# A stacked fp16 null-value product and a three-pass fp16 decay product in a two-layer gated cross-attention kernel

## What is computed

```
# block 1: attention over 256 context rows and one null row
nk = jnp.broadcast_to(null_kv[0], (b, HEADS, 1, DH))
nv = jnp.broadcast_to(null_kv[1], (b, HEADS, 1, DH))
k = jnp.concatenate((nk, k), axis=-2)
v = jnp.concatenate((nv, v), axis=-2)
attn = jax.nn.softmax(jnp.einsum('bhid,bhjd->bhij', q * scale, k), axis=-1)
out = jnp.einsum('bhij,bhjd->bhid', attn, v)
out = jnp.einsum('bnf,fd->bnd', out.transpose(0, 2, 1, 3).reshape(b, -1, INNER), Wout)
...
# block 3: a first-order recurrence over the context rows, then a pick by the token's boundary count
a = jnp.exp(dt[:, :, None] * A[None, None, :])
u = (dt * bcoef)[:, :, None, None] * x4
_, s = jax.lax.associative_scan(comb, (a_b, u), axis=1)
depool_out = depool[jnp.arange(bsz)[:, None], plug]
h = jnp.einsum('bld,ed->ble', rmsnorm(embeds, g_res), W_in) + b_in
return depool_out + h
```

## Time and profile before

| | |
|---|---|
| median of three runs | 1682.9 us (1676.08 to 1683.25) |
| the profiled execution | 1678.45 us, span of the core 1676.7 us |
| TensorE (PE) busy | 1493.0 us, 89% |
| VectorE (DVE) busy | 1195.3 us, 71% |
| ScalarE (ACT) busy | 922.1 us, 55% |
| GpSimd (POOL) busy | 589.2 us, 35% |
| mean granted TensorE clock | 0.964 of full |
| one full step | 74.4 us (ScalarE's copy of p0T at 510.76, 585.17, 659.53 us) |

### The profile page before, as it was taken

The page is one execution under the profiler, slowest core; times in us unless marked ns, Lnnn a source line. Parts: engine busy times, 40 slices in busy tenths (PEclk is TensorE's granted clock), DMA queues, the critical chain, the costliest instruction groups (busy, mean ns, idle before and its releaser), DMA issues.

```text
span 1676.7 us, 35791 instructions
## 1 busy us (share of the span) xinstructions
PE 1493.0 (89%) x12510; PEld 1085.1 (65%) x12510; DVE 1195.3 (71%) x3240; ACT 922.1 (55%) x2526; POOL 589.2 (35%) x775
## 2 busy tenths in 40 slices
PE   3799999999999999999999999999765499999994
PEld 2567676767767676767767676776553266666662
DVE  5478788888878888887978888887763344445442
ACT  4276666767666676767666676766641133333331
POOL 3011333242323333232333324232333356555552
PEclk9899999999999999999999999999877699999997
DMA  7201021020202012020201102010400363333334
GB/s 249 70 1 64 14 64 58 20 77 2 77 8 71 26 52 71 7 76 1 77 14 64 65 14 77 2 58 8 164 32 0 105 173 61 60 59 58 58 61 123
DMA packets 77836, 98.12 MB, mean 59 GB/s; under 512 B 20400, under 2 KB 61376, under 8 KB 77600
## 3 DMA queue, kind: packets, MB, share of 16 engines
q1 hardware_dynamic: 51152, 77.01, 14.1%
q0 software_dynamic: 15680, 18.69, 6.8%
q10 hardware_dynamic: 10832, 0.13, 0.3%
HBM read 64.89 MB, written 35.10 MB: 60 GB/s over the span
## 4 chain that ended last, share of the span: by engine, by line
PE 62%; DVE 18%; ACT 7%; POOL 5%; issue 3%; SPq 2%; DMA 2%; ACTq 0%; POOLq 0%; DVEq 0%
PE S L1282 11%; PE W L949 9%; PE W L951 9%; PE W L950 9%; PE T L954 7%; PE O L1302 6%; PE O L1053 4%; POOL routing_table L693 4%; PE S L1027 3%; DVE mx L1462 3%; ACT prob L785 2%; DVE pTl L1474 2%; PE W L954 2%; PE W L1158 2%; PE W L1138 2%
## 5 line engine op out<-in xcount | busy, mean ns | idle before, releaser
L785 ACT ACTIVATE prob<-S,nm 128x256 f32<-128x256 f32 x512 | 235.5, 474 | 80.8 <-DVE nm L1465 54.1
L778 ACT ACTIVATE pTh<-T 128x512 f16<-128x512 f32 x256 | 139.3, 597 | 137.1 <-PE T L954 136.9
L634 POOL TENSOR_SCALAR ve_ln<-mv_ln 128x2 f32<-128x2 f32 x64 | 14.6, 229 | 472.8 <-DVE mv_ln L1436 471.9
L1462 DVE TENSOR_REDUCE mx<-S 128x2 f32<-128x512 f32 x256 | 163.3, 679 | 21.2 <-PE S L1027 20.7
L1282 PE MATMUL S<-GL,xgh 128*128 x568 | 169.8, 381 | 2.7 <-DVE xgl L1756 2.7
L1474 DVE SCALAR_TENSOR_TENSOR pTl<-T,pTh 128x512 f16<-128x512 f32 x256 | 164.1, 682 | 6.4 <-ACT pTh L778 6.4
L716 POOL DMA_INDIRECT acc_rows<-ysb,tab x71 | 112.3, 1582 | 134.2 <-DMA acc_rows<-ysb,tab 90.3
L794 ACT ACTIVATE prob<-prob,rden 128x256 f32<-128x256 f32 x256 | 116.5, 504 | 56.4 <-DVE p0n L1483 55.7
L954 PE MATMUL T<-ident,prob 128*128 128x128 f32 x1024 | 141.5, 282 | 1.8 <-DVE prob L1487 1.7
L949 PE MATMUL W<-cTh,Wkh 128*128 128x256 f16 x512 | 140.6, 275 | 0.0
L950 PE MATMUL W<-cTl,Wkh 128*128 128x256 f16 x512 | 140.5, 274 | 0.0
(11 more groups left out here) (293 smaller groups left out, 4325.1 us busy)
## 6 DMA issues: line engine op xcount, KB each, us to landing
cx<-in_ctx_dram SPq DMA_DIRECT2D x16, 512.0 KB
gst<-in_L_ffn_gating_w_dram SPq DMA_DIRECT2D x16, 512.0 KB
gating_split<-gsp SPq DMA_DIRECT2D x16, 512.0 KB
GL<-gating_split SPq DMA_DIRECT2D x8, 1024.0 KB
stg<-in_L_xattn_Wkv_dram SPq DMA_DIRECT2D x8, 512.0 KB, 13.5
xl<-in_x_dram SPq DMA_DIRECT2D x16, 256.0 KB
lst<-in_L_ffn_linear_w_dram SPq DMA_DIRECT2D x16, 256.0 KB
xres<-in_x_dram SPq DMA_DIRECT2D x16, 256.0 KB
```

Of the source, the lines that this page charges most:

```text
L778: A(flat(pTh[:, h, :, :]), T[h][:, :], ACT.Copy).then_inc(s_pTh[h], 1)
L785: ins = A(prob[:, h, t, :], S[h][:, t * NTOK:(t + 1) * NTOK], ACT.Exp, bias=nm[:, h, t:t + 1], scale=SM, accum_out=rs[:, h, t:t + 1])
L1462: ins = V.tensor_reduce(mx[:, h, :], S[h][:, :].rearrange("p (t k) -> p t k", t=TT), AX.X, ALU.max)
```

## The change

It does five things.

1. **Null product.** `Wnv` and `p0T` become fp16 with 96 rows: in rows 0, 32 and 64 start the high, low and high probabilities, against the high, high and low of Wnv. One fp16 matmul does what the fp32 product did. `p0n` has its 16 columns three times (96 wide, zeros between), the transposes give 96 rows, ScalarE copies all 96 rounded to fp16, and VectorE then overwrites rows 32 to 47 with the remainder. The bank is now freed by VectorE.
2. **Decay product.** `dec` and `u` are split into fp16 high and low by GpSimd (two instructions each, per batch), and the fp32 products become `mm3`. win_unit waits for the splits.
3. `u` is one buffer; its split goes into two pairs of buffers. VectorE waits for the former split before it writes `u`.
4. `x4` shares the buffer of `xh`, `x4T` that of `xn`. VectorE's wait for the former x4 rows' DMA moves from j = 7 to j = 2.
5. In setup: larger zero fills on GpSimd, four more small VectorE copies, and `Wnv` made by two VectorE instructions in place of one.

```
-         ("p0T", False, POST)
+         ("p0T", True, POST)
...
+                    wait_apart(pool, s_gt, post.n + 1)
+                    link(pool.tensor_copy(dech[:, :, :], dec[:, :, :]))
+                    pool.tensor_tensor(decl[:, :, :], dec[:, :, :], dech[:, :, :], ALU.subtract).then_inc(s_gts, 1)
                     rstd_of("ln4", post, 1e-5).then_inc(s_rstd["ln4"], 1)
                     wait_apart(pool, s_rstd["ln4"], post.n + 1)
                     rms_of_normed("ln4", 1e-6).then_inc(s_rms, 1)
+                if PRE in parts:
+                    wait_apart(pool, s_u, nxt.n + 1)
+                    link(pool.tensor_copy(uh[nxt.par][:, :, :], u[:, :, :]))
+                    pool.tensor_tensor(ul[nxt.par][:, :, :], u[:, :, :], uh[nxt.par][:, :, :], ALU.subtract)\
+                        .then_inc(s_us, 1)
...
                     if j == 0 and post_:
-                        whole("p0T", p0T[:, :])
+                        one_of("p0T", p0T[:, :])
...
-                        ins = tr(o[0:HEADS, t * P:(t + 1) * P], p0n[post.par][:, t, :])
+                        ins = tr(o[0:NULL_ROWS, t * P:(t + 1) * P], p0n[post.par][:, t, :])
...
-                    pe.wait_ge(s_gt, post.n + 1)
-                    pe.wait_ge(s_u, post.n + 1)
+                    pe.wait_ge(s_gts, post.n + 1)
+                    pe.wait_ge(s_us, post.n + 1)
...
-                            ins = M(o[:, c], dec[:, k, tok], u[post.par][:, k, :], start=False, stop=(k == 1))
+                            ins = mm3(o[:, c], dech[:, k, tok], decl[:, k, tok], uh[post.par][:, k, :],
+                                      ul[post.par][:, k, :], False, k == 1)
...
-            V.tensor_scalar(Wnv[:, :], banks_of[12][0:HEADS, 0:D], WS, None, ALU.mult).then_inc(s_init, 1)
+            link(V.tensor_scalar(Wnv[:, :], banks_of[12][0:NULL_ROWS, 0:D], WS, None, ALU.mult))
+            V.scalar_tensor_tensor(Wnv[64:64 + HEADS, :], banks_of[12][64:64 + HEADS, 0:D], WS, Wnv[64:64 + HEADS, :],
+                                   ALU.mult, ALU.subtract).then_inc(s_init, 1)
...
                     if j == 2 and post_:
+                        dve.wait_ge(s_x4o, 16 * (post.n + 1))
...
                     if attn:
                         divide(j)
 
+                    if j == 0 and post_:
+                        k, _, nhalf = work.at["p0T"][0]
+                        dve.wait_ge(half[k], nhalf)
+                        V.scalar_tensor_tensor(p0T[32:32 + HEADS, :], W[k][32:32 + HEADS, 0:NTOK], 1.0,
+                                               p0T[32:32 + HEADS, :], ALU.mult, ALU.subtract).then_inc(free[k], 1)
```

More of the change, by code:

```diff
@@ L45 @@
 PRE, ATTN, POST = "pre", "attn", "post"
-UNITS = [("p0T", False, POST), ("ctxT", True, PRE), ("ctxT", True, PRE), ("wout", False, POST),
+UNITS = [("p0T", True, POST), ("ctxT", True, PRE), ("ctxT", True, PRE), ("wout", False, POST),
          ("xT", True, PRE), ("k", True, PRE), ("q", True, PRE), ("q", True, PRE),
@@ L55 @@
 NWORK = 3
+NULL_ROWS = 96
 LOOP_START, LOOP_STEPS = 2, NB - 4
@@ L154 @@
 POOL_CHUNKS = (4, 6)
-POOL_STEPS = 18
+POOL_STEPS = 20
 XG, YS, TB = 6, 6, 8
@@ L217, in build @@
         Wnh, Wnl = sb("Wnh", [P, KD, HEADS], FP16), sb("Wnl", [P, KD, HEADS], FP16)
-        Wnv = sb("Wnv", [HEADS, D])
+        Wnv = sb("Wnv", [NULL_ROWS, D], FP16)
         rw = sb("rw", [P, KD, E])
@@ L230, in build @@
         tokid = sb("tokid", [P, TT], I32)
+        p0n = [sb(f"p0n{i}", [P, TT, NULL_ROWS]) for i in range(2)]
         phase.append(ExitStack())
@@ L244, in build @@
         neg = sb("neg", [P, 2, NB])
-        nvsel = sb("nvsel", [P, KF, HEADS])
+        nvsel = sb("nvsel", [P, KF, NULL_ROWS])
         fillt = sb("fillt", [P, TABLE_COLS, 2], I32)
@@ L266, in build @@
         ns0 = [sb(f"ns0{i}", [P, TT, HEADS]) for i in range(2)]
-        u = [sb(f"u{i}", [P, TT, D]) for i in range(2)]
+        u = sb("u", [P, TT, D])
+        uh, ul = [sb(f"uh{i}", [P, TT, D], FP16) for i in range(2)], [sb(f"ul{i}", [P, TT, D], FP16) for i in range(2)]
         sq = sb("sq", [P, TT, CTX], FP16)
@@ L278, in build @@
         rden = sb("rden", [P, 2, TT])
-        p0n = [sb(f"p0n{i}", [P, TT, HEADS]) for i in range(2)]
-        p0T = sb("p0T", [HEADS, NTOK])
+        p0T = sb("p0T", [NULL_ROWS, NTOK], FP16)
         pTh, pTl = sb("pTh", [P, 2, 2, NTOK], FP16), sb("pTl", [P, 2, 2, NTOK], FP16)
@@ L296, in build @@
         dec = sb("dec", [P, 2, NTOK])
+        dech, decl = sb("dech", [P, 2, NTOK], FP16), sb("decl", [P, 2, NTOK], FP16)
         x3 = sb("x3", [P, TT, D])
-        x4 = sb("x4", [P, TT, D])
-        x4T = sb("x4T", [P, KD, NTOK])
+        x4 = xh
+        x4T = xn
         st = {n: sb("st_" + n, [P, TT, 6]) for n in ("ln1", "lno", "ln2", "ln3", "ln4")}
@@ L397, in build @@
         s_ol = sem("attn_low")
-        s_u = sem("u_ready")
+        s_u, s_us = sem("u_ready"), sem("u_split")
         s_xb = sem("xres_biased")
@@ L404, in build @@
         s_dec = sem("decay_exp")
-        s_gt = sem("decay_ready")
+        s_gt, s_gts = sem("decay_ready"), sem("decay_split")
         s_ms = sem("experts_selected")
@@ L611, in _ @@
             link(pool.iota(rowno[:, :], pattern=[[1, TABLE_COLS]], base=0, channel_multiplier=TABLE_COLS))
+            for n in range(2):
+                link(pool.memset(p0n[n][:, :, :], 0.0))
             pool.memset(fillt[:, :, :], 0).then_inc(s_pre, 1)
@@ L801, in whole, with one_of @@
                     A(dst, W[k][0:dst.shape[0], 0:dst.shape[1]], ACT.Copy).then_inc(free[k], 1)
+                def one_of(name, dst):
+                    k, nfull, _ = work.at[name][0]
+                    act.wait_ge(full[k], nfull)
+                    A(dst, W[k][0:dst.shape[0], 0:dst.shape[1]], ACT.Copy).then_inc(half[k], 1)
                 def q_high(m):
@@ L995, in _ @@
             for f in range(KF):
-                ins = M(banks_of[12][0:HEADS, 0:D], nvsel[:, f, :], stg[CHUNKS - 2 + f // 4][:, (f % 4) * D:(f % 4 + 1) * D],
+                ins = M(banks_of[12][0:NULL_ROWS, 0:D], nvsel[:, f, :], stg[CHUNKS - 2 + f // 4][:, (f % 4) * D:(f % 4 + 1) * D],
                         start=(f == 0), stop=(f == KF - 1))
@@ L1345, in _ @@
             V.tensor_copy(lensT[:, :, :].rearrange("p a b -> p (a b)"), banks_of[1][:, 0:2 * NB]).then_inc(s_udve, 1)
[L1346 to L1349, removed]
+            every, last = NULL_ROWS + 2, (NULL_ROWS + 2) * (KF - 1) + 1
+            for part in range(2):
+                r = slice(64 * part, 64 * part + 64)
+                for at in range(part, NULL_ROWS, 32):
+                    ins = V.tensor_copy(nvsel[r, :, :].rearrange("p a b -> p (a b)")[:, at:at + last:every],
+                                        nvc[r, :].broadcast_to([64, KF]))
+            ins.then_inc(s_nvsel, 1)
             V.tensor_scalar(gres64[:, :], gresc[:, :], WS, None, ALU.mult).then_inc(s_udveg, 1)
@@ L1482, in divide @@
                     link(V.reciprocal(rden[:, :, :], den[:, :, :]))
-                    V.tensor_tensor(p0n[i.par][:, :, 2 * j:2 * j + 2].rearrange("p t h -> p h t"), p0[:, :, :],
-                                    rden[:, :, :], ALU.mult).then_inc(s_rden, 1)
+                    V.tensor_tensor(p0n[i.par][:, :, :].rearrange("p t (r s) -> p r s t", s=32)[:, :, 2 * j:2 * j + 2, :],
+                                    p0[:, :, :].unsqueeze(1).broadcast_to([P, NULL_ROWS // 32, 2, TT]),
+                                    rden[:, :, :].unsqueeze(1).broadcast_to([P, NULL_ROWS // 32, 2, TT]),
+                                    ALU.mult).then_inc(s_rden, 1)
                     for t in range(TT):
@@ L1693, in step @@
                         if post_:
-                            dve.wait_ge(s_x4o, 16 * (post.n + 1))
                             normed("ln4", post, x4, tiles(x3), rstd["ln4"]).then_inc(s_nrm["ln4"], 1)
@@ L1697, in step @@
                             dve.wait_ge(s_rstd["ctx"], nxt.n + 1)
+                            at_least(dve, s_us, nxt.n)
                             for t in range(TT):
-                                ins = V.scalar_tensor_tensor(u[nxt.par][:, t, :], cx[nxt.par][:, t, 0:D], rc[:, t:t + 1],
+                                ins = V.scalar_tensor_tensor(u[:, t, :], cx[nxt.par][:, t, 0:D], rc[:, t:t + 1],
                                                              gi_b[:, :], ALU.mult, ALU.mult)
```

## The result

The changed kernel takes **1769.4 us** (median of 4 runs, 1767.33 to 1770.23), the kernel before, run beside it, 1681.6 us. The ratio is 1.0527 (95% interval 1.0508 to 1.0546). The profiled execution took 1769.36 us with a span of 1767.6 us.

The account below looks back on a forecast made before the run. TensorE, busy 89%, was taken to bound the batch steps. A full step: +3.7 - 0.43 + 2.2 = +5.5 us, 14 making +77; with ends and setup +82 on 1678.45, 1760, put at 1762 us; range 1725 to 1788.

Parts of the forecast that it names:

- Stall: TensorE ahead of wout: waits for bank W0, freed by VectorE behind divide(0); stands still 6.0 us per full step.
- Null product: On TensorE, an fp16 matmul replaces the fp32 product: 0.83 us becomes 0.27, saving 1.1 us per step; wider transposes cost nothing.
- The rule of four passes: Skill's rule for the fp32 null product: 0.44 us, saving 0.33 per product; set aside for the profile row's 0.83 us.
- Clock: Behind each stall ahead of wout the clock falls to 0.50, costing 1.6 to 3.2 us; 2.2 taken.
- Rival A: The stall ahead of wout is there but the clock stays up: +49, 1729 us; chance 14%.
- What comes back: At j = 1, TensorE's waits for xn, pTl and xTl vanish: 1.2 us per step.
- Decay product: Between win and scores(7), six fp16 matmuls replace two fp32 products: saves 0.43 us per step.
- Splits on GpSimd: GpSimd's splits of dec and u take 1.8 us each, covered ahead of win and the scatter: cost nothing.
- The ends: Outside the middle steps: step 15 +5.4 us, step 16 -1.3, setup +0.4.
- Rival C: W0's release does not hold up wout, so only the savings count: 24 us less, 1659 us; chance 2%.
- Rival D: VectorE's new instruction stands ahead of divide(0): stall 2.9 us, +0.2 a step, 1682 to 1715 us; chance 2%.

Follow-up runs that it names:

- Runs 1 to 3: Wait alone on the kernel before: 1778.7 us; on the changed kernel, low null rows behind maxima(0): 1706.4 us, ahead of maxima(0): 1690.3 us.
- run 4: Changed kernel with 48 fp16 matmuls, whose results nobody reads, ahead of wout's wait: 1746.3 us, ratio 1.0394.
- run 7: Changed kernel with low null rows made by GpSimd ahead of the transposes, ScalarE's copy freeing the bank: 1674.5 us; a second kernel adds one more edit.
- run 2: Changed kernel with VectorE's low null rows instruction moved behind maxima(0), ahead of divide(0): 1706.4 us, ratio 1.016.
- Runs 6 and 9: 6: split of u a step later on changed kernel, 1765.4 us; 9: bias sum xb waits for xn, on run 7's first kernel 1668.3 us, kernel before 1672.2 us.
- the second kernel of run 7: Changed kernel with low null rows made by GpSimd ahead of the transposes and the split of u a step later: 1688.5 us, ratio 1.0041.

## Why the prediction was right, point by point

The sign, the mechanism and the place were right; 1762 us was 7 short of 1769, and the measurement lies inside the range. That a step comes out so close (5.5 forecast, 5.8 measured) is in part luck: a hold-up of 0.87 us that the prediction put at nothing, and 0.24 more stall, stand against 0.54 more that came back and 0.21 less for the clock.

- **Stall.** Forecast 6.0 us, measured 6.24. `divide(0)` ended when it should. The instruction took the 0.42 us of its nearest row, but the overlap of 0.08 was not there and TensorE took 0.14 us to start, not 0.06. The idle row that the prediction puts at about 6 us is 4.8 to 5.2: the transposes ahead of wout, costed at nothing, end later and lie within the 6.24. Runs 1 to 3 show that this place alone makes the stall.
- **Null product.** Forecast -1.1, measured -1.13 (wout at full clock in runs 4 and 7). The row decided rightly. The rule of four passes (the Trainium skill, FP8 and Floating Point Precision, TensorE Precision Notes) gives -0.66 as an estimate.
- **Clock.** Forecast 2.2 us per stall, measured 7.55 - 5.56 = 1.99. Rival A, the clock stays up, is out by the windows and by run 4: there 23 us came back, more than the 17 us that I had worked out from the sentence on a ramp under 1% of a typical kernel's span (the Trainium skill, TensorE: Matmul & The Clock Gate, Part 1). That sentence does not speak of a kernel with a stall in every step, and as a bound for one it did not hold.
- **What comes back.** Forecast -1.2, measured -1.60 at j = 1 (0.55 ahead of xn's transposes, 0.46 ahead of values(0), 0.58 ahead of q) and -0.14 further on.
- **Decay product.** Forecast -0.43, measured -0.43.
- **Splits on GpSimd.** Forecast nothing ("Both cost nothing"). **This step failed**: +0.87 us a step, some 12 us in all. The time stayed inside the range because the step is small. I had asked who waits for the splits, and there the answer holds (win was not delayed). I had not asked which VectorE instructions run beside what the splits push later. It is also why the kernel's own loss at xn hid from me: xn takes about 1.55 us in the kernel before too, and I took that for its price.
- **The ends.** Steps 1 and 15 lost 7.4 and 6.6 us where 5.5 and 5.4 were forecast, and the rest of the program 1.4 more where -1.3 was. I did not take these apart; their causes stay open.
- **Rival C** would not have given 1659 us. Without the stall the null product's saving goes into the wait for xn (run 7), so 1674.5 is what "only the savings count" gives, and 1688 if GpSimd's splits lie badly.
- **Rival D**, priced at 1682 to 1715, was run 2: 1706.

## What to carry to other kernels

When a bank, a buffer or a semaphore changes the engine that frees it, price the change by where that engine's program stands, not by the instruction: 0.42 us of work cost 5 us of idleness here, and ahead of the first maxima 0.4 to 0.8. Before an engine's saving is booked, look at what it will wait for next, since 1.13 us on TensorE vanished to the hundredth in the wait for xn. Work put on an "idle" GpSimd must be laid beside VectorE's timeline, including every instruction that it pushes later.

## What the runs showed of the hardware

A VectorE instruction that reads only SBUF can stand still until a GpSimd cast, sum or subtraction beside it has ended: msel 0.17 to 1.01 us, `d` 0.14 to 1.13, `dl` 0.16 to 0.81, xn 0.74 to 1.55, idf 0.17 to 0.42. Runs 6 and 9 took the GpSimd work away from beside msel and xn, and the hold-up was gone; the second kernel of run 7 put it beside `d`, and `d` was held. The ends agree within 0.03 us for msel, `d` and idf. VectorE instructions that read PSUM (mx, pTl, the statistics of W) kept their time beside the same GpSimd work, and so did the aggregation of one small SBUF input (0.25 us). Not every overlap costs: `u`, a product of two SBUF inputs of 256 columns, took 0.88 us for its two instructions beside GpSimd's 2-column work, as long as `x`, which has the same shape and reads PSUM (0.87).

The Trainium skill has this rule, SBUF — State Buffer, Who interferes with whom: VectorE shares a port pair with GpSimd; a VectorE operation with two SBUF inputs contends for it with a GpSimd operation that reads SBUF, one in a two-port mode contends too, and whoever issues first has it for the whole instruction while the other blocks. The traces agree for msel, `d` and `dl`, which have two SBUF inputs, with the numbers above. Whether xn and idf, with one, ran in a two-port mode no run shows, nor does any row here show GpSimd standing behind VectorE.

Filling the stall with idle matmuls kept the granted clock at 1.00 (run 4), but such a fill has to end before the wait does: here it ended 0.34 us too late.
